# Graph network kernel on one core: the waits in front of the four row gathers of an edge chunk are exchanged

## The chip, the cores and the metric

The kernel runs on one core of one Trainium2 chip. The metric is the device time of one execution in microseconds (us). The kernel before takes 4315.86 us, the median of three runs (4311.51 to 4329.4).

## The reference

The model has four graph layers over 3125 nodes of 128 features and 50000 edges sorted by their end node. The change touches the first one, and of it the part that is computed for each edge. Cut to that part:

```python
x_src = node_features[src]
h = silu(edge_attr @ fc1 + b1);  h = silu(h @ fc2 + b2);  scale = h @ fc3 + b3
msg = silu(x_src @ W_node * scale + edge_sh @ W_sh)
alpha_in = concatenate([x_src[:, :64], node_features[dst, :64], edge_attr], -1)
a = silu(alpha_in @ aW1 + ab1);  a = silu(a @ aW2 + ab2);  a = a @ aW3 + ab3
```

The softmax over the edges, the sums over the edges of a node and the three later layers follow in later phases. They are not touched.

## The kernel before, in words

`edge_messages` is one phase of the kernel. It handles the edges in 100 chunks of 512 (`CE`), and four buffers (`U` = 4) hold the chunks in flight. An earlier phase has already computed, for every node, one row of 256 numbers in DRAM: `x @ W_node` and `x[:, :64] @ aW1[:64]`. For each chunk GpSimd copies the 512 edge ends from `idx` into `slot` (line 983, the operand named `em_idx`) and then issues four indirect DMAs (line 998), each of which gathers 128 rows of 1 KB into `gs[:, u, j]`, j = 0 to 3. They are called gather 0 to gather 3 here. Each raises `rows_in[u]`.

The other engines go through the chunks in turns. In turn c TensorE runs these steps in this order:

- `begin(c)`: the first edge layer FC1 (line 1021), the edge part of the score layer (1022), the product SH of the chunk before (1014), the part of the end nodes (1028) and the transposes of the gathered halves (1034), which complete the sum A1.
- `counts`: in one or two places of a turn six matmuls of line 1070, which count edges between node blocks for a later layer. Two turns in four have them twice, two once.
- `finish(c-1)`: SCALE (1043) and the score product A3 (1049).
- `middle(c)`: FC2 (1060) and A2 (1062). Then the scores of chunk c-1 are transposed (1055), then come the second `counts`.

ScalarE applies the four activations H1, A1, H2 and A2 (all at line 1106), the message MSG (1120) and the copies of the counts (1127). VectorE copies the scores out of PSUM (1189, `em_a`), and then adds b3 (TB, 1190), multiplies by the gathered rows (TG, 1193, the step after which `gs[:, u]` is free) and adds SH (TS, 1196). Beside that it builds one-hot matrices for the counts (1246, 1247). In the first 64 chunks it also splits 16 pieces of another edge input (1210, 1214).

Every step raises a semaphore. `early` is raised by TensorE after FC1, A1, FC2 and A2, `late` by TensorE after SH, SCALE and A3, `act_` by ScalarE after H1, A1, H2 and A2, `dve_` by VectorE after TB, TG, TS and the last score step, `scores_ok` by VectorE after line 1189. `X.of(c, "NAME")` is the value that the semaphore has once step NAME of chunk c is done. The next turn of TensorE begins when ScalarE has finished A2 of the chunk:

```python
def begin(c, u, i, fast, first=False):
    pe.wait_ge(feat_in[u // 2], (i + 1) * 48)
    pe.wait_ge(act_.sem, act_.of(c - 1, "A2"))
```

Each engine executes its instructions in order, so a wait on GpSimd holds up whatever gathers stand behind it. Nothing but the index copies and the gathers is on GpSimd in this phase. SyncE issues all the other DMAs of the phase from a queue of its own and waits for nothing that GpSimd does. `both` runs `body(True)` for inputs like these ("fast"); `body(False)` is a general path that is not executed here.

Of the kernel before, what the change touches and what calls it, by code (L numbers as in the profile page):

```python
# [782 lines left out]
def edge_messages(k, idx, a_all, first_, tops):  # L783
# [4 lines left out]
    U, NWI, NHI = NCU, NWU, NWU * NH  # L788
    EW_, SHW = 2 * EA, 2 * EA + SH
    pieces, step = PIECES, EW // GQ // PIECES  # L790
    with k.phase("em") as (sb, sem, block, hop):
# [20 lines left out]
        early = Steps(sem("early"), ["FC1", "A1", "FC2", "A2"], U)  # L812
        late = Steps(sem("late"), ["SH", "SCALE", "A3"], U)
        scores_turned = Steps(sem("scores_turned"), ["A3"], U)
        scores_ok = Steps(sem("scores_ok"), ["A3"], U)
        cleared, topped = sem("cleared"), sem("topped")
        act_ = Steps(sem("act"), ["H1", "A1", "H2", "A2"], U)
        act_msg = Steps(sem("act_msg"), ["MSG"], U)
# [4 lines left out]
        dve_ = Steps(sem("dve"), ["TB", "TG", "TS", "A3"], U)  # L823
        HB, AB, SCALE, SHB, A3, ADJ, HB2 = 0, 1, 2, 3, 4, 5, 7
# [19 lines left out]
        def both(eng, body):  # L844

            with eng.If(eng.value_load(k.fits[0:1, 0:1], min_val=0, max_val=1) == 1):
                body(True)
            with eng.If(eng.value_load(k.fits[0:1, 0:1], min_val=0, max_val=1) == 0):
                body(False)
# [125 lines left out]
        @block.gpsimd  # L975
        def _(pool):
            def body(fast):
                with pool.Fori(0, NC // U) as i:
                    for u in range(U):
                        c = U * i + u  # L980
                        pool.wait_ge(early.sem, early.of(c - U, "A1"))
                        pool.sem_inc(hop["pool"], 1)
                        nc.gpsimd.tensor_copy(slot[:, u, :].unsqueeze(1), idx[:, bass.ds(c, 1), :]).then_inc(indexed.sem, 1)
                        pool.wait_ge(dve_.sem, dve_.of(c - U, "TG"))
                        pool.sem_inc(hop["pool"], 1)
                        pool.wait_ge(indexed.sem, indexed.of(c, "IDX"))
                        pool.sem_inc(hop["pool"], 1)
                        for j in range(4):
                            if fast and j == 1:
                                pool.wait_ge(act_msg.sem, act_msg.of(c - U, "MSG"))  # L990
                                pool.sem_inc(hop["pool"], 1)
                            if fast and j == 2:
                                pool.wait_ge(act_.sem, act_.of(c - U + 2, "H1"))
                                pool.sem_inc(hop["pool"], 1)
                            if fast and j == 3:
                                pool.wait_ge(scores_ok.sem, scores_ok.of(c - U + 1, "A3"))
                                pool.sem_inc(hop["pool"], 1)
                            pool.indirect_dma_start(out=gs[:, u, j, :], out_offset=None, in_=d["rows0"],  # L998
                                                    in_offset=bass.IndirectOffsetOnAxis(ap=slot[:, u, 2 * j:2 * j + 1], axis=0)
                                                    ).then_inc(rows_in[u], 16)  # L1000
                            if not fast:
                                pool.indirect_dma_start(out=gd[:, u, j, :], out_offset=None, in_=d["rows0d"],
                                                        in_offset=bass.IndirectOffsetOnAxis(ap=slot[:, u, 2 * j + 1:2 * j + 2], axis=0)
                                                        ).then_inc(rows_in[u], 16)

            indexed.prime(pool)
            both(pool, body)

        @block.tensor
# [3202 lines left out]
```

## Time and profile before

| | |
|---|---|
| median of three runs | 4315.86 us |
| the profiled execution, its own time | 4329.4 us |
| its span, from the first to the last instruction | 4327.6 us |
| TensorE clock granted, mean of the span | 0.916 of full speed |
| the phase `edge_messages` | from 83 to 890 us of the span |

The profile is of one execution, the slowest of the three. Its own time is 1.8 us more than its span. Times in the rows below are microseconds from the start of the span. In a row of the timeline the bracket at the end gives how long the engine had been idle before the instruction, and what ended that idle time; "remote" and "issue" mean that the profile names no instruction. PE is TensorE, ACT is ScalarE, DVE is VectorE, POOL is GpSimd. The end of a PE row is modelled, and a row of several matmuls ("x8") gives the start of the first.

### The profile page before, as it was taken

The page shows a single profiled execution, that of the slowest core. Times are in us where ns is not written, and L with a number is a line of the kernel's source. Part 1 is how long each engine was busy: PE and PEld are TensorE (multiplying, and loading weights), DVE is VectorE, ACT ScalarE, POOL GpSimd, SP SyncE. Part 2 cuts the span into 40 slices and gives each one's busy share as a digit, 9 for nine tenths or more (in the row PEclk, how much of TensorE's full clock was granted, in tenths as well). Part 3 has the DMA queues.
Part 4 walks back from the last instruction along what each step waited for, and adds up shares of the span by engine and source line. Part 5 has one row for each costly group of instructions (what it writes and reads, how often), then busy time and mean ns, then how long its engine had stood idle before and what let it go on. Part 6 is the DMA issues. An engine that isn't in the chain of part 4 may idle for free. (4 is left out here: it accounts for less than half of the span.)

```text
span 4327.6 us, 82914 instructions
## 1 busy us (share of the span) xinstructions
PE 3495.6 (81%) x22381; PEld 2067.5 (48%) x22381; DVE 1823.4 (42%) x5369; ACT 1433.0 (33%) x3483; POOL 1862.8 (43%) x1907
## 2 busy tenths in 40 slices
PE   4999999947758888876777777667777769999998
PEld 2666666635534444443444444334443444555564
DVE  4666666647523333332333333323333323344222
ACT  3555555522623333332233323222222223122112
POOL 2555555500256665653566656456666630000000
PEclk8999999979879999998888998878898889999999
DMA  5677775656444554555666666556666645443223
GB/s 139 187 200 199 198 196 167 165 115 204 140 136 137 140 136 131 139 137 136 169 176 172 176 175 179 156 155 167 167 164 168 166 111 176 171 177 118 74 97 125
DMA packets 716528, 675.29 MB, mean 156 GB/s; under 512 B 382359, under 2 KB 542945, under 8 KB 716117
## 3 DMA queue, kind: packets, MB, share of 16 engines
q1 hardware_dynamic: 622598, 466.26, 37.1%
q0 software_dynamic: 77008, 200.24, 17.2%
q10 hardware_dynamic: 16768, 6.91, 0.6%
q8 instruction: 76, 1.25, 0.1%
q14 instruction: 78, 0.64, 0.0%
HBM read 530.84 MB, written 142.28 MB: 156 GB/s over the span
## 5 line engine op out<-in xcount | busy, mean ns | idle before, releaser
L2293 POOL DMA_INDIRECT l_y<-s_lrows,l_src x1344 | 1352.6, 1006 | 964.3 <-issue 352.4
L2373 PE MATMUL ps<-l_y,aw_pT 128*63 128x277 f32 x2700 | 436.8, 467 | 259.9 <-ACT aw_pT L2591 249.1
L3404 PE MATMUL ps<-nl_adj,nl_table 126*128 126x504 bf16 (+1 forms) x3150 | 631.4, 357 | 2.3 <-DVE nl_table L3639 2.3
L998 POOL DMA_INDIRECT em_gs<-s_rows,em_idx x400 | 432.3, 1081 | 325.8 <-DVE em_a L1189 147.9
L2357 PE MATMUL ps<-aw_yT,aw_qt 128*63 128x384 f32 x1800 | 377.2, 529 | 120.0 <-DMA aw_yT<-s_dxT 61.2
L3404 PEld LDWEIGHTS ps<-nl_adj,nl_table 126*128 126x128 bf16 x3150 | 301.8, 96 | 299.0 <-issue 5.3
L2750 DVE COPY aw_axd<-ps 128x252 f32<-128x252 f32 x225 | 94.7, 421 | 796.9 <-remote 409.9
L2330 PE MATMUL ps<-ident,l_y 128*128 128x128 f32 x1800 | 281.5, 292 | 150.9 <-issue 83.1
L2373 PEld LDWEIGHTS ps<-l_y,aw_pT 128*63 128x63 f32 x2700 | 195.7, 154 | 431.9 <-ACT aw_pT L2591 279.6
L2591 ACT ACTIVATE aw_pT<-ps 128x381 f32<-128x381 f32 x225 | 109.9, 488 | 736.8 <-remote 506.0
L2577 ACT ACTIVATE aw_yT<-ps 128x512 f32<-128x512 f32 (+1 forms) x525 | 261.4, 536 | 245.2 <-remote 114.7
L2330 PEld LDWEIGHTS ps<-ident,l_y 128*128 128x128 f32 x1800 | 220.5, 150 | 202.3 <-issue 124.5
L2730 DVE TENSOR_REDUCE aw_mx<-ps 127x1 f32<-127x384 f32 x225 | 124.5, 553 | 396.9 <-remote 333.0
L2599 ACT ACTIVATE aw_agr<-ps,aw_inv 127x277 f32<-127x277 f32 x225 | 111.0, 494 | 440.4 <-PE ps L2373 200.0
L2357 PEld LDWEIGHTS ps<-aw_yT,aw_qt 128*63 128x63 f32 x1800 | 108.8, 148 | 239.5 <-issue 92.0
L2715 DVE TENSOR_TENSOR l_y<-l_y 128x768 f32<-128x768 f32 x225 | 212.4, 944 | 24.1 <-issue 14.4
L1106 ACT ACTIVATE em_h<-ps,ei_bias 128x512 f32<-128x512 f32 x200 | 136.3, 682 | 147.3 <-PE ps L1060 79.0
L1247 DVE TENSOR_SCALAR em_oh_key<-ei_iota_key,em_key 128x546 bf16<-128x546 int16 x450 | 165.7, 368 | 0.0
L1106 ACT ACTIVATE em_a<-ps,ei_bias 128x512 f32<-128x512 f32 x200 | 137.2, 686 | 72.8 <-PE ps L1034 26.0
L2365 PEld LDWEIGHTS ps<-ident,aw_p 127*128 127x128 f32 x675 | 73.7, 147 | 145.1 <-issue 144.3
L2584 ACT ACTIVATE aw_p<-ps,aw_neg 127x384 f32<-127x384 f32 x225 | 132.4, 589 | 31.6 <-DVE aw_neg L2733 16.4
L1189 DVE COPY em_a<-ps 104x128 f32<-104x128 f32 x100 | 29.2, 292 | 251.0 <-remote 182.5
(381 smaller groups left out, 5866.1 us busy)
## 6 DMA issues: line engine op xcount, KB each, us to landing
nl_adj<-s_adj SPq DMA_DIRECT2D x20, 3100.8 KB
aw_yT<-s_dxT SPq DMA_DIRECT2D x150, 384.0 KB
aw_geoS<-s_geoS SPq DMA_DIRECT2D x450, 94.5 KB
nl_adj<-s_adj SPq DMA_DIRECT2D x15, 2325.6 KB
ws_msg<-s_msg SPq DMA_DIRECT2D x75, 384.0 KB, 3.8
s_dxT<-aw_yT SPq DMA_DIRECT2D x75, 384.0 KB
aw_qt<-s_qt SPq DMA_DIRECT2D x225, 126.0 KB
s_msg<-em_msg SPq DMA_DIRECT2D x100, 256.0 KB
```

Of the source, the lines that this page charges most:

```text
L998: pool.indirect_dma_start(out=gs[:, u, j, :], out_offset=None, in_=d["rows0"], in_offset=bass.IndirectOffsetOnAxis(ap=slot[:, u, 2 * j:2 * ...
L1106: nc.scalar.activation(to[:, u % 2, :], k.ps[:, bank, :], ACT.Silu, bias=bias[:, col:col + 1]).then_inc(act_.sem, 1)
L1247: nc.vector.tensor_scalar(oh_key[:, o, j, :], iota_key[:, :], key[:, v, q:q + 1], None, ALU.is_equal).then_inc(s, 1)
L2293: pool.indirect_dma_start(out=y[:, u, j, 0:W], out_offset=None, in_=table, in_offset=bass.IndirectOffsetOnAxis(ap=src[:, u, j:j + 1], axis ...
L2330: m = nc.tensor.transpose(k.ps[:, FEATURES[n], q * 128:(q + 1) * 128], y[:, u, j, what * D:(what + 1) * D], k.ident[:, :])
L2357: m = nc.tensor.matmul(rows_(v), qt[:, u, v, t, :], yT[:, SLOT[u], t, v * HS:(v + 1) * HS], start=False, stop=t == 1)
L2373: m = nc.tensor.matmul(k.ps[64 * v:64 * v + HW, SUM, 0:SW], pT[:, SLOT[u], j, 64 * v:64 * v + HW], y[:, u, v * TH + j, 0:SW], start=j == 0 ...
L2577: nc.scalar.activation(yT[:, SLOT[u], :, :].rearrange("p t s -> p (t s)")[:, n * 512:n * 512 + size], k.ps[:, FEATURES[n], 0:size], ACT.Co ...
L2584: nc.scalar.activation(p[:, SLOT[u], :], k.ps[0:M, SCORE[u], 0:HS], ACT.Exp, bias=neg[:, u:u + 1], scale=SCALE, accum_out=den[:, u:u + 1]) ...
L2715: nc.vector.tensor_tensor(y[:, u, :, D:2 * D], y[:, u, :, W - D:W], bc(y[:, u, :, G0:G0 + 1], [128, T, D]), ALU.mult).then_inc(ready.sem, 1)
L2730: nc.vector.tensor_reduce(mx[:, u:u + 1], k.ps[0:M, SCORE[u], 0:HS], AX.X, ALU.max).then_inc(s, 1)
L3404: m = nc.tensor.matmul(k.ps[:, bank(i, p), 0:cols * WN], source[:, p, q, b, :], adj[:, a % 2, 0:cols, b * WN:(b + 1) * WN], start=b == 0 a ...
```

## The change

The loop over the chunks on GpSimd keeps its index copy and its four gathers. What they wait for changes:

| in front of | before | after |
|---|---|---|
| the index copy of chunk c | A1 of c-4 (TensorE) | TG of c-4 (VectorE) |
| gather 0 | TG of c-4, own copy | own copy, H2 of c-3 (ScalarE) |
| gather 1 | MSG of c-4 (ScalarE) | nothing |
| gather 2 | H1 of c-2 (ScalarE) | FC1 of c-2 (TensorE) |
| gather 3 | the score copy of c-3 (VectorE, line 1189) | A1 of c-2 (TensorE) |

```diff
                         c = U * i + u
-                        pool.wait_ge(early.sem, early.of(c - U, "A1"))
+                        pool.wait_ge(dve_.sem, dve_.of(c - U, "TG"))
                         pool.sem_inc(hop["pool"], 1)
                         nc.gpsimd.tensor_copy(slot[:, u, :].unsqueeze(1), idx[:, bass.ds(c, 1), :]).then_inc(indexed.sem, 1)
-                        pool.wait_ge(dve_.sem, dve_.of(c - U, "TG"))
-                        pool.sem_inc(hop["pool"], 1)
                         pool.wait_ge(indexed.sem, indexed.of(c, "IDX"))
                         pool.sem_inc(hop["pool"], 1)
+                        if fast:
+                            pool.wait_ge(act_.sem, act_.of(c - U + 1, "H2"))
+                            pool.sem_inc(hop["pool"], 1)
                         for j in range(4):
-                            if fast and j == 1:
-                                pool.wait_ge(act_msg.sem, act_msg.of(c - U, "MSG"))
-                                pool.sem_inc(hop["pool"], 1)
                             if fast and j == 2:
-                                pool.wait_ge(act_.sem, act_.of(c - U + 2, "H1"))
+                                pool.wait_ge(early.sem, early.of(c - U + 2, "FC1"))
                                 pool.sem_inc(hop["pool"], 1)
                             if fast and j == 3:
-                                pool.wait_ge(scores_ok.sem, scores_ok.of(c - U + 1, "A3"))
+                                pool.wait_ge(early.sem, early.of(c - U + 2, "A1"))
                                 pool.sem_inc(hop["pool"], 1)
```

## Rows read from the trace of the kernel before

**Rows 1.** The page: the span, and TensorE's busy time, share and instructions.
```profile
span 4327.6 us, 82914 instructions
...
PE 3495.6 (81%) x22381; PEld 2067.5 (48%) x22381; DVE 1823.4 (42%) x5369; ACT 1433.0 (33%) x3483; POOL 1862.8 (43%) x1907
```

**Rows 2.** Busy time by stretch of 100 us: each engine, then clock, DMA share, GB/s.
```profile
750.00:850.00 100.00, 98.50 (x648) 63.59 (x647) 65.89 (x231) 52.19 (x84) 58.14 (x64) 1.00 0.58 168
```

**Rows 3.** The source line 1189: count, ns min/median/max, first and last start.
```profile
L1189 DVE COPY em_a<-ps x100: 291/292/293, 104.3 to 886.7; 104x128 f32<-104x128 f32 x100
```

**Rows 4.** Timeline of one turn amid the phase: start, us, engine, line [idle before].
```profile
813.46 0.29 DVE L1189 COPY em_a<-ps 104x128 f32<-104x128 f32 x1 [3.65 <-remote]
...
814.38 0.69 DVE L1193 TENSOR_TENSOR em_t<-em_t,em_gs 128x512 f32<-128x512 f32 x1
814.54 1.36 POOL L998 DMA_INDIRECT em_gs<-s_rows,em_idx  x1 [1.81 <-DVE em_a L1189]
...
814.82 0.69 PE L1021 MATMUL ps<-ei_feat,ei_fc 32*128 32x512 f32 x1
...
815.90 0.20 POOL L983 COPY em_idx<-idx_all 128x8 int32 x1
...
816.89 1.16 POOL L998 DMA_INDIRECT em_gs<-s_rows,em_idx  x1 [0.79 <-ACT em_msg L1120]
...
817.16 1.06 PE L1034 MATMUL ps<-ident,em_gs 128*128 128x128 f32 x8
...
818.25 0.69 ACT L1106 ACTIVATE em_a<-ps,ei_bias 128x512 f32<-128x512 f32 x1 [0.59 <-PE ps L1034]
...
818.35 1.09 POOL L998 DMA_INDIRECT em_gs<-s_rows,em_idx  x1 [0.30 <-issue]
...
819.74 0.95 POOL L998 DMA_INDIRECT em_gs<-s_rows,em_idx  x1 [0.30 <-issue]
...
819.75 0.41 PE L1049 MATMUL ps<-em_a,ei_aw 128*8 128x128 f32 x8
...
820.08 1.13 PE L1060 MATMUL ps<-em_h,ei_fc 128*128 128x512 f32 x2
...
821.37 0.29 DVE L1189 COPY em_a<-ps 104x128 f32<-104x128 f32 x1 [2.31 <-PE ps L1049]
...
821.41 0.69 ACT L1106 ACTIVATE em_h<-ps,ei_bias 128x512 f32<-128x512 f32 x1 [0.23 <-PE ps L1060]
...
822.85 0.69 PE L1021 MATMUL ps<-ei_feat,ei_fc 32*128 32x512 f32 x1
```

**Rows 5.** Timeline of a turn after the last gather of the phase (869.41).
```profile
869.99 0.66 PE L1021 MATMUL ps<-ei_feat,ei_fc 32*128 32x512 f32 x1
...
873.92 0.41 PE L1049 MATMUL ps<-em_a,ei_aw 128*8 128x128 f32 x8
...
874.25 1.12 PE L1060 MATMUL ps<-em_h,ei_fc 128*128 128x512 f32 x2
...
874.39 0.29 DVE L1189 COPY em_a<-ps 104x128 f32<-104x128 f32 x1 [2.05 <-PE ps L1049]
...
875.42 0.69 ACT L1106 ACTIVATE em_h<-ps,ei_bias 128x512 f32<-128x512 f32 x1 [1.59 <-PE ps L1060]
...
877.11 0.66 PE L1021 MATMUL ps<-ei_feat,ei_fc 32*128 32x512 f32 x1
```

**Rows 6.** Timeline of the second turn of the phase.
```profile
97.05 0.69 PE L1021 MATMUL ps<-ei_feat,ei_fc 32*128 32x512 f32 x1 [0.78 <-ACT em_a L1106]
...
101.06 0.41 PE L1049 MATMUL ps<-em_a,ei_aw 128*8 128x128 f32 x8
...
104.32 0.29 DVE L1189 COPY em_a<-ps 104x128 f32<-104x128 f32 x1 [9.48 <-remote]
```

**Rows 7.** Timeline of a turn in which VectorE also splits a piece.
```profile
404.53 0.71 DVE L1210 TENSOR_TENSOR em_edge_left<-ei_edge,em_edge_part 126x536 f32<-126x536 f32 x1
...
404.61 0.66 POOL L983 COPY em_idx<-idx_all 128x8 int32 x1
```

## The prediction

> **What bounds the kernel now.** The page comes first: TensorE is busy for 81% of the span [rows 1]. That is a mean over phases; the change lies in one phase, so the next view is the busy time by stretch. In the middle of the phase TensorE is busy for 98.5 of 100 us at a granted clock of 1.00, which is the 2.4 GHz level [rows 2]. By that row alone the phase is bound by TensorE, the gathers have no part in it, and the change could do nothing. But ends of PE rows are modelled, so I look at who receives TensorE's results. The score copy, line 1189, runs 100 times from 104.3 to 886.7 us [rows 3]: one turn in 782.4/99 = 7.90 us.
>
> The timeline of one turn shows what fills the 7.9 us [rows 4]. TensorE starts the score product, line 1049, at 819.75, and VectorE's copy of it starts at 821.37, 1.62 us later. TensorE starts FC2, line 1060, at 820.08, a third of a microsecond after, and ScalarE's H2 starts at 821.41, 1.33 us later. Two results that TensorE made one after the other arrive 0.04 us apart. In a turn without gathers the same two steps take 874.39-873.92 = 0.47 us and 875.42-874.25 = 1.17 us [rows 5]. So beside a row of gathers the completions of TensorE are seen late, the scores by 1.15 us, FC2 by 0.16 us in this turn. The turn itself is shorter without gathers: from line 1021 to line 1021 877.11-869.99 = 7.12 us [rows 5] against 822.85-814.82 = 8.03 us [rows 4]. The latter has one set of count matmuls more, some 0.7 us, so 0.2 us of it is the delay; in the turn ahead of it, without the additional set, far more is.
>
> The third thing to see is when they arrive: 821.37 is 0.68 us after the end of the last gather of a close row of three (818.35, 819.74 and the one at 816.89), 819.74+0.95 = 820.69 [rows 4]. And a row of gathers that is longer delays more: in the second turn of the phase, where all semaphores are still primed and GpSimd issues without pause, line 1049 starts at 101.06 and the copy at 104.32, 3.26 us later [rows 6]. A1, whose last transposes start at 817.16 before the second gather of the row, reaches ScalarE at 818.25, at once [rows 4]. My reading: a completion of TensorE that falls into the second or a later gather of a close row is held until some 0.7 us after the last one ends, or slips through between. Three turns is a small basis for the mechanism, but it closes a loop whose sum fits: copy start to gather 3 1.08 us (814.54-813.46), gather 1.36, index copy 0.20, hand-over 0.79, gathers 0 to 2 with their gaps 1.16+0.30+1.09+0.30+0.95 = 3.80, hold 0.68, together 7.91 us, and the next copy does start 7.91 us later (821.37-813.46) [rows 4]. GpSimd's own chain sets the turn, with 1.4 us of it in waits that it makes itself.
>
> At one point the Trainium skill speaks against this. Its page "SBUF — State Buffer", section "Who interferes with whom", says that only the port pair of VectorE and GpSimd causes contention and that TensorE and ScalarE wait for nobody. By that rule the gathers can't touch TensorE's turn and the sum of the change is nothing; by the rows it is what follows. The 1.15 us disagree with the rule for completions, if not for the matmuls themselves, and I follow the rows but leave the rule a chance.
>
> **The change, part by part.** Take the turn that starts at 814.82. TG, line 1193, ends at 814.38+0.69 = 815.07 [rows 4].
>
> 1. Gather 3 no longer waits for the score copy. Before it started 1.08 us after the copy and took 1.36 us beside line 1193 instead of the 0.95 us of another gather: 0.41 us of GpSimd's time comes back, and it is in the chain.
> 2. The index copy now waits for TG instead of A1 of four chunks ago. A1 was long done; TG ends 1.61 us after the score copy starts. So the chain has 1.61 us where it had 1.08, and the hand-over from TG to the index copy comes on top. No row shows this one. The bounds are 0 and the 0.79 us that a gather needs after what it waited for; the index copy is a short operation that follows without a DMA to prepare, so I take 0.3 us, nearer the lower.
> 3. The index copy was behind the gather and beside line 1210 in the 16 turns that split a piece: 0.66 us there instead of 0.20 [rows 7]. It now stands beside line 1196, which reads one of its inputs from PSUM. If it is undisturbed, 16 x 0.46 = 7 us are saved; if line 1196 holds it up as line 1210 did, all 96 turns cost 0.46 us more, 44 us. I take the saving.
> 4. H2 of c-3 in front of gather 0: it ends 0.69 us after its start and starts with the score copy [rows 4], before TG does. Nothing, plus at most 0.1 us for one more wait. The wait for MSG that goes was met already (gap 0.30 us before 818.35). FC1 for H1 at gather 2: both long done. Nothing either way, and their cover is the whole row of gathers.
> 5. Gather 3 waits for A1 of c-2, the transposes of line 1034 in the turn that is running. Now 0.30 us after gather 2 it would be ready if A1 has been seen. The four gathers then form one close row.
>
> The row would start at 815.07+0.3+0.20+0.79 = 816.36 and run 3.80 us to gather 2's end at 820.16, and with gather 3 (0.30+0.95) to 821.41. A3 of this turn (819.75 and 0.47) and FC2 fall inside, so both are held to 821.41+0.68 = 822.09. The new chain from score copy to score copy is 1.61+0.3+0.20+0.79+3.80+1.25+0.68 = 8.63 us against 7.91, +0.72 us a turn. With the bounds of step 2 it is 8.33 to 9.12. That is a **joined** turn.
>
> But A1 is a completion of TensorE too. Its transposes start at 817.16 and it is due at 818.25 [rows 4]. The second gather of the new row would start at 816.36+1.16+0.30 = 817.82, so A1 is due inside it and may be held. If it slips through by about 819.7, gather 3 joins. If not, it is freed at 820.16+0.68 = 820.84, and A3 with it, 0.53 us earlier than today; gather 3 starts another 0.79 us later, alone. FC2 is then not held at all. That is a **split** turn. Its lower bound is a turn without gathers: 7.12 us with one set of counts and about 7.8 with two, mean 7.48 against 7.90, -0.42. Since A1 itself comes late for ScalarE I take -0.3 us.
>
> Nothing else is behind the waits: GpSimd holds only the next gathers, and TensorE needs chunk c+3's rows some 11 us after they are issued, so late rows are no price. The number of turns is 96, from chunk 4 on; the first four are primed and nearly unchanged.
>
> **The forecast.** A joined turn releases scores and FC2 together, which puts the next TG late in its turn and A1 deep into the row: likely held. A split turn releases the scores early, TG comes early, A1 falls near the first gather and is seen at once: joined. So I expect both kinds in turn, somewhat more joined (11 in 20), since one that slips through is enough. 0.55 x 0.72 - 0.45 x 0.3 = +0.26 us a turn, x 96 = +25 us, less 7 us from step 3: +18 us. The profiled execution goes from 4329.4 to 4347 us. It lies 13.5 us above the median of the runs, so the median goes from 4315.9 to 4334 us.
>
> **The rivals.**
>
> - *Always joined.* A1 slips through each time, as completions in close rows sometimes must for the sum to close. 0.72 x 96 - 7 = +62 us: 4378 us. For it: the second turn of the phase, 3.26 us. Against: A1 is due half a microsecond into the second gather.
> - *Always split* (the other side). The place is gather 3 behind A1; it decides as soon as A1 is seen later than 0.79 us before gather 2's end plus the hold, about 820.1. -0.3 x 96 - 7 = -36 us: 4280 us, with the bound of -0.42 4268 us. For it: A3 in rows 4 was held for 1.15 us, and A1 held as long would be seen at 819.4, not far off. Against: a turn whose A1 is prompt ends it.
> - *No change.* TensorE's queue, 98.5% busy [rows 2], is the bound after all and late completions only show where it has slack. Then 4316 us, or 4309 with step 3. The page named above would give this case. Against: the 7.12 us turn.
> - *A blocked index copy.* With 44 us on top of the forecast 4385 us; unlikely, since it needs line 1196 to block.
>
> **How the numbers follow.** A measurement of this kernel tells about 0.5%, 21.6 us, from no change. Chances: mixed 0.30, always joined 0.24, always split 0.25, no change 0.17, blocked copy 0.04. The mixed case with shares from 0.4 to 0.7 joined runs from 4319 to 4348 us, so I split it into 0.03 faster, 0.15 within and 0.12 slower. Faster 0.28, within 0.32, slower 0.40. The likeliest case's own range is 4312 to 4355 us. The range for 8 in 10 reaches to both rivals: 4268 (split at its bound) to 4385 us.
>
> **What would show it.** The start of line 1189 against line 1049, per turn: over 2 us in joined turns, under 1.2 in split ones; below 0.5 everywhere would mean that the new places avoid the hold entirely. The mean turn, first to last start of line 1189 over 99: 8.1 to 8.2 for the forecast, 8.6 joined, 7.5 split, 7.9 no change. GpSimd: four gathers with gaps of 0.30 us, or a gap above 0.9 us before the fourth. Gather 3 at 0.95 us, not 1.36, shows step 1; an index copy of 0.20 us in all turns, step 3. A turn that is long although scores are prompt would show that my loop is the wrong one.

## The result and the profile after

The changed kernel takes 4390.31 us (median of 4 executions, 4382.59 to 4400.81) where the kernel before takes 4322.63 us (4 executions on the same chip). The ratio is 1.016, 95% interval 1.0124 to 1.0196: **slower by 1.6%**, outside the range of 4268 to 4385 us and on the side to which I had given 0.40. The profiled execution took 4409.3 us, with a span of 4407.5 us.

All line numbers of the phase behind 985 are two lower now: the gathers are 996, the score copy is 1187. Three views answer to [rows 1, 3]: the busy times of the page, two groups of the lines (busy us, mean ns, idle time before, and what ended it), and the score copy's line by itself (shortest, median and longest in ns, first and last start in us).

```profile
PE 3495.3 (79%) x22381; PEld 2087.8 (47%) x22381; DVE 1826.6 (41%) x5369; ACT 1429.6 (32%) x3483; POOL 1819.9 (41%) x1907
```

```profile
L996 POOL DMA_INDIRECT em_gs<-s_rows,em_idx x400 | 400.5, 1001 | 247.2 <-issue 86.0 <-PE ps L1058 59.9 <-ACT em_a L1104 46.5
L983 POOL COPY em_idx<-idx_all 128x8 int32 x100 | 19.1, 191 | 227.2 <-DVE em_t L1191 157.3 <-DVEq L69 55.8 <-issue 14.0
```

```profile
L1187 DVE COPY em_a<-ps x100: 291/292/293, 107.5 to 939.4; 104x128 f32<-104x128 f32 x100
```

TensorE is busy for the same 3495 us [rows 1]; nothing was added to its work. The score copy now runs from 107.5 to 939.4 us, one turn in 831.9/99 = 8.40 us instead of 7.90. That is 50 us of the loss, the whole of what the change can have done: in the attention phase, whose code is the same, the profiled execution of after took 29 us longer (2313.5 us against 2284.1 from the first to the last matmul of its line 2371, before 2373), but over the 14 profiled executions in this study with late reports that phase took 2284 to 2331 us, whatever the kernel. For the rest of the span, which I use below as a cleaner measure beside the ratio, before has 4327.6-2284.1 = 2043.5 us and after 2094.0 us.

A mean turn of 8.40 us hides two patterns. Cut at turn 67 (TensorE's FC1 to FC1, turn 0 is the first): in turns 2 to 66 the mean is 8.77 us where before has 7.98; in turns 68 to 97 it is 7.73, and before has 7.85. The windows show the granted clock of the two parts, from turn 3 to 66 and from 69 to 97 (window, length, busy us of PE, PEld, DVE, ACT and POOL, clock, DMA share, GB/s):

```profile
118.69:680.18 561.49, 511.46 (x3265) 336.80 (x3265) 348.23 (x1166) 274.95 (x447) 270.87 (x319) 0.94 0.64 180
698.81:923.36 224.55, 206.00 (x1484) 139.98 (x1483) 149.18 (x517) 116.35 (x190) 120.02 (x144) 0.98 0.61 169
```

This is the slow pattern, from the timeline of one joined turn. It began at 360.90 (line 1019) and the next at 369.78, so 8.88 us:

```profile
361.32 0.19 POOL L983 COPY em_idx<-idx_all 128x8 int32 x1 [2.96 <-DVE em_t L1191]
362.45 0.97 POOL L996 DMA_INDIRECT em_gs<-s_rows,em_idx  x1 [0.94 <-POOL em_idx L983]
363.16 1.06 PE L1032 MATMUL ps<-ident,em_gs 128*128 128x128 f32 x8
363.73 1.05 POOL L996 DMA_INDIRECT em_gs<-s_rows,em_idx  x1 [0.31 <-issue]
364.25 0.69 ACT L1104 ACTIVATE em_a<-ps,ei_bias 128x512 f32<-128x512 f32 x1 [0.60 <-issue]
365.08 0.95 POOL L996 DMA_INDIRECT em_gs<-s_rows,em_idx  x1 [0.30 <-issue]
365.74 0.41 PE L1047 MATMUL ps<-em_a,ei_aw 128*8 128x128 f32 x8
366.33 0.95 POOL L996 DMA_INDIRECT em_gs<-s_rows,em_idx  x1 [0.30 <-issue]
368.42 0.29 DVE L1187 COPY em_a<-ps 104x128 f32<-104x128 f32 x1 [2.57 <-remote]
...
370.28 0.19 POOL L983 COPY em_idx<-idx_all 128x8 int32 x1 [3.01 <-DVE em_t L1191]
```

A1 (line 1032, 363.16) reaches ScalarE 1.09 us later, at once; so gather 3 starts with the 0.30 us gap of an unhindered row, and the score product started at 365.74 is copied 2.68 us later. From one index copy to the next are 8.96 us: the next turn looks much the same (there A1 is seen after 2.25 us, still ahead of gather 2's end). All of this is from one profiled execution of each kernel. And this is the other pattern, a split turn of the last third, from 824.04 to 831.68 = 7.64 us:

```profile
824.58 0.99 POOL L996 DMA_INDIRECT em_gs<-s_rows,em_idx  x1 [0.94 <-ACT em_a L1104]
825.46 1.06 PE L1032 MATMUL ps<-ident,em_gs 128*128 128x128 f32 x8
825.88 1.07 POOL L996 DMA_INDIRECT em_gs<-s_rows,em_idx  x1 [0.30 <-issue]
827.25 1.10 POOL L996 DMA_INDIRECT em_gs<-s_rows,em_idx  x1 [0.30 <-issue]
828.05 0.40 PE L1047 MATMUL ps<-em_a,ei_aw 128*8 128x128 f32 x8
829.04 0.69 ACT L1104 ACTIVATE em_a<-ps,ei_bias 128x512 f32<-128x512 f32 x1 [3.15 <-remote]
829.30 0.29 DVE L1187 COPY em_a<-ps 104x128 f32<-104x128 f32 x1 [1.76 <-PE ps L1047]
829.79 0.95 POOL L996 DMA_INDIRECT em_gs<-s_rows,em_idx  x1 [1.44 <-PE ps L1058]
830.22 0.69 DVE L1191 TENSOR_TENSOR em_t<-em_t,em_gs 128x512 f32<-128x512 f32 x1
```

Here A1 is seen only 829.04-825.46 = 3.58 us later, 0.69 us behind the end of the third gather, and gather 3 comes apart. In turns 26, 52 and 78 GpSimd pauses for some 3 us ahead of gather 1, in every kernel here that has four gathers; these turns and the ones behind them (27, 53, 79) are left out of all counts of joined turns below. Of the other turns from 2 to 66, 47 have four gathers in a row (gather 3 less than 1.95 us behind gather 2), with a mean of 9.06 us; of those from 68 to 97 none has (78 and 79, at the pause, do).

With the turns at the pauses counted in, there are twelve stretches of joined turns. Eleven begin in a turn in which VectorE does the second subtraction of an edge piece, the twelfth at the pause in turn 78. One of the eleven:

```profile
415.68 0.69 PE L1019 MATMUL ps<-ei_feat,ei_fc 32*128 32x512 f32 x1
416.12 0.70 DVE L1212 TENSOR_TENSOR em_edge_part<-em_edge_left,em_edge_part 126x536 bf16<-126x536 f32 x1
416.21 1.45 POOL L996 DMA_INDIRECT em_gs<-s_rows,em_idx  x1 [0.94 <-ACT em_a L1104]
417.10 1.06 PE L1032 MATMUL ps<-ident,em_gs 128*128 128x128 f32 x8
417.97 1.13 POOL L996 DMA_INDIRECT em_gs<-s_rows,em_idx  x1 [0.30 <-issue]
418.19 0.69 ACT L1104 ACTIVATE em_a<-ps,ei_bias 128x512 f32<-128x512 f32 x1 [0.67 <-issue]
```

Gather 0 started 0.09 us behind the subtraction and took 1.45 us instead of 0.97 to 1.10. The second gather then starts late, A1 is seen at once, 0.22 us behind its start, and gather 3 joins. Of turns 3 to 97, 18 have a gap of over 1.6 us between the starts of gathers 0 and 1 (the three pauses among them), and in all 18 A1 is seen 1.09 us behind its transposes. The Trainium skill, page "SBUF — State Buffer", section "Who interferes with whom", says that a VectorE instruction with two inputs in SBUF contends with a GpSimd instruction that reads SBUF, and that the order of issue decides who is blocked. The trace agrees with the contention and with one side of the order: in [rows 4] a gather that started 0.16 us behind line 1193 took 1.36 us, and in the split turn above one that started 0.43 us ahead of the same operation took 0.95 us. The other side it doesn't show: VectorE's operation, which came second there (830.22), took the same 0.69 us as ever.

The last thing in the trace is the clock. Nine of turns 2 to 97 take over 10 us, eight of them up to turn 67; before has none. One is the turn from 396.93 to 408.18 (the windows of the turn before it, its own and the next):

```profile
387.95:396.93 8.98, 7.64 (x50) 4.66 (x49) 4.06 (x13) 4.21 (x7) 4.07 (x5) 1.00 0.48 143
396.93:408.18 11.25, 11.25 (x55) 7.95 (x54) 7.52 (x24) 4.48 (x8) 4.29 (x6) 0.70 0.55 152
408.18:415.68 7.50, 6.58 (x50) 4.38 (x49) 4.96 (x21) 4.14 (x8) 4.10 (x5) 1.00 0.60 175
```

After joined turns, in which TensorE is busy for only 7.64 of 8.98 us, the granted clock falls, for part of a turn, from the 2.4 to the 1.2 GHz level (0.70 is the mean of this one), and the turn takes 2.2 us more than a joined one does in the mean. Counted so, the nine turns are 20 us of the 50, an estimate. Such a turn mostly ends the pattern: here, as after most of them, the next is split. In turns 2 to 97 the clock stands at the 1.2 GHz level for 83 us of the changed kernel and for 9 us of before.

### The profile page after: what moved, and what is told of

The parts are those of the page before. It is cut to its first block and busy times, and to the rows that moved or that the text cites. A ratio compares the mean times of both kernels' runs of the same rounds, so it can differ in the third digit from the quotient of the medians.

```text
span 4407.5 us, 82939 instructions
## 1 busy us (share of the span) xinstructions
PE 3495.3 (79%) x22381; PEld 2087.8 (47%) x22381; DVE 1826.6 (41%) x5369; ACT 1429.6 (32%) x3483; POOL 1819.9 (41%) x1907
## 3 DMA queue, kind: packets, MB, share of 16 engines
q10 hardware_dynamic: 16768, 6.91, 0.6%
## 5 line engine op out<-in xcount | busy, mean ns | idle before, releaser
L2371 PE MATMUL ps<-l_y,aw_pT 128*63 128x277 f32 x2700 | 445.8, 475 | 287.7 <-ACT aw_pT L2589 283.9
L996 POOL DMA_INDIRECT em_gs<-s_rows,em_idx x400 | 400.5, 1001 | 247.2 <-issue 86.0
```

What stands on the lines that cost most here:

```text
L2371: m = nc.tensor.matmul(k.ps[64 * v:64 * v + HW, SUM, 0:SW], pT[:, SLOT[u], j, 64 * v:64 * v + HW], y[:, u, v * TH + j, 0:SW], start=j == 0 ...
```

## The experiments

The ratio is to the kernel before on the same chip, with its 95% interval. "Turn" is first to last score copy over 99. "Rest" is the profiled span without the attention phase. The first twelve ran where before takes 4328 to 4373 us; kernels 13 to 16 (13 was run three times) where it takes 3766 to 3768 us, more on that below. Turn and rest are of one profiled execution each. The times in my expectations for kernels 1 to 4 reckon with a before of 4323 us; where they ran it takes 4363 us.

| kernel | ratio | turn, us | rest, us |
|---|---|---|---|
| before | | 7.90 | 2043.5 |
| changed | 1.016 (1.0124-1.0196) | 8.40 | 2094.0 |
| 1 index copy behind TG alone | 1.000 (0.9985-1.0014) | 7.95 | 2048.5 |
| 2 gather 3 behind A1 alone | 0.9979 (0.9961-0.9996) | 7.79 | 2034.0 |
| 3 changed, short subtractions | 1.0027 (1.0008-1.0046) | 8.13 | 2062.5 |
| 4 changed, gather 3 behind FC2 | 0.9973 (0.9951-0.9994) | 7.85 | 2041.0 |
| 5 before, gather 3 behind FC2 | 0.9975 (0.996-0.9991) | 7.88 | 2043.6 |
| 6 parts 1 and 2 together | 0.9971 (0.9951-0.9992) | 7.80 | 2034.1 |
| 7 changed, no piece work | 1.0024 (1.0007-1.0041) | 8.04 | 2059.2 |
| 8 before, one gather a chunk | one execution, 4260.6 us | 6.77 | 1930.7 |
| 9 changed without the H2 wait | 0.9963 (0.9942-0.9985) | 7.70 | 2025.5 |
| 10 changed with H1 for FC1 | 1.0147 (1.0117-1.0177) | 8.48 | 2096.4 |
| 11 part 6 and a wait for MSG | 1.0326 (1.0287-1.0364) | 9.28 | 2176.3 |
| 12 part 2 without the MSG wait | 0.9988 (0.9957-1.0018) | 7.80 | 2035.4 |
| 13 as 9, one passed wait | 0.9996 (0.9973-1.0019) | 6.91 | 1925.5 |
| 14 as 9, three passed waits | 1.0014 (0.9993-1.0035) | 6.97 | 1930.8 |
| 15 as 9, gather 3 behind FC2 | 0.9985 (0.9968-1.0002) | 7.00 | 1932.7 |
| 16 as 9, rows of two | 0.9998 (0.9976-1.0019) | 6.99 | 1932.2 |

**The parts alone (1 and 2).** Kernel 1 is before with the two waits exchanged around the index copy:

```diff
-                        pool.wait_ge(early.sem, early.of(c - U, "A1"))
+                        pool.wait_ge(dve_.sem, dve_.of(c - U, "TG"))
...
-                        pool.wait_ge(dve_.sem, dve_.of(c - U, "TG"))
-                        pool.sem_inc(hop["pool"], 1)
```

> The kernel before with one part of the change alone: the index copy waits for the product TG and no longer for A1; the gathers keep their old waits. Theory H (TensorE's completion reports are held while gathers follow each other closely, and gather 3 in the same row as gathers 0 to 2 makes the row long): gather 3 still waits for the score copy and stands apart, so the phase keeps turns of 7.8 to 8.1 us and the time is 4310 to 4345 us. Rival C (the index copy and its hand-over, now in series behind TG, lengthen the chain by themselves): turns of about 8.4 us as in the changed kernel, 4365 to 4395 us.

Kernel 2 is before with

```diff
-                                pool.wait_ge(scores_ok.sem, scores_ok.of(c - U + 1, "A3"))
+                                pool.wait_ge(early.sem, early.of(c - U + 2, "A1"))
```

> The kernel before with another part alone: gather 3 waits for the matmul A1 of two chunks back in place of the score copy of three chunks back; index copy and gathers 0 to 2 as before. Theory H: gather 3 follows gather 2 by 1.3 us, rows of four, score copy 2.7 to 3.4 us behind its matmul, turns of 8.2 to 9.0 us, 4350 to 4430 us. Rival C (index copy): gather 3 merely comes earlier, no turn is longer than before, at or below 4323 us.

Kernel 1 made no difference, so the index copy in series is not by itself the loss (rival C falls). Kernel 2 was a miss for my theory as it then stood: rows of four do occur, in 36 of turns 2 to 66, with a mean of 8.30 us, but never in more than three turns on end, and in turns 68 to 97 the turn is 7.34 us. Gather 3 behind A1 is by itself a small gain.

**The edge pieces (3 and 7).** Kernel 3 is the changed kernel with the two subtractions on 8 of 536 columns; the others hold zeros:

```diff
-                nc.vector.tensor_tensor(edge_left[:, :], edge[:, :], edge_part[:, 0, :], ALU.subtract)
+                nc.vector.tensor_tensor(edge_left[:, 0:8], edge[:, 0:8], edge_part[:, 0, 0:8], ALU.subtract)
...
-                nc.vector.tensor_tensor(edge_part[:, 2, :], edge_left[:, :], edge_part[:, 1, :], ALU.subtract)
+                nc.vector.tensor_tensor(edge_part[:, 2, 0:8], edge_left[:, 0:8], edge_part[:, 1, 0:8], ALU.subtract)
```

> The changed kernel with VectorE's two subtractions of the edge pieces done on 8 of their 536 columns (work left out: two of the three parts of the edge features are zero elsewhere). Theory H with two patterns: in the changed kernel one of these subtractions delays gather 1 by 0.45 us, which lets A1's report through early, joins gather 3 to the row, and the pattern of four then keeps itself up. Without them the split pattern of the last 30 turns (7.64 us) holds in nearly all 98: 4280 to 4310 us. Rival C: nothing of the kind, the phase stays at 8.4 us a turn but for 16 times 0.7 us, 4370 to 4390 us. Rival D (TensorE's lower clock in these stretches is the cause, not the result): stretches at the lower clock stay, above 4350 us.

Kernel 7 is kernel 3 with ScalarE's two copies of a piece cut in the same way:

> The changed kernel with all four operations of the edge pieces, VectorE's two and ScalarE's two, on 8 of 536 columns (work left out: the split edge features are zero elsewhere). Theory H2: nothing but the missing gathers at turns 26 and 78 starts the pattern of four; it ends by itself; turns of 7.64 us in over 85 of 98, 4325 to 4350 us beside a before of about 4363. Rival (the pattern of four comes from something else that recurs, a store or a table load): about the 4376 us that VectorE's two alone gave.

With no change to a wait, the ratio fell from 1.016 to 1.003: joined turns went from 48 to 25 of 90, with all piece work short to 20. So the subtractions start most of the joined stretches of the changed kernel. But nothing of the kind is needed: both forecasts of a nearly clean phase were missed, and in kernel 7 stretches of joined turns also began in turns 13, 37, 66, 86 and others, where I found no operation that starts them. Eight of kernel 3's joined turns, and eight of kernel 7's, lie behind turn 67, where the changed kernel, with the same instructions there, has none; so that its last third was clean is in part luck.

**Gather 3 behind a later event (4 and 5).** The wait for A1 in the changed kernel (4), or for the score copy in before (5), becomes

```diff
+                                pool.wait_ge(early.sem, early.of(c - U + 2, "FC2"))
```

> The changed kernel with gather 3 behind the matmul FC2 of two chunks back in place of A1. Theory H: FC2's report always falls behind the row of three, so gather 3 never joins it, edge pieces or not; turns of 7.6 to 7.9 us, 4285 to 4325 us. Rival C: 4370 to 4395 us, as the index copy stands where it stood.

> The kernel before with gather 3 behind the matmul FC2 of two chunks back in place of the score copy; the index copy stays ahead of TG. Theory H2 (held reports; gather 0 directly behind TG with the copy already done, three gathers in a row, gather 3 apart in every turn because FC2's report always comes behind the row): turns near the 7.2 us that the same kernel with A1 in place of FC2 showed where it was not joined, in the edge-piece turns too: 4295 to 4330 us beside a before of about 4363 on this chip. Rival: FC2's report comes so late that gather 3 runs into the next gather 0; then 4 in a row again and 4355 to 4400 us.

Kernel 4 has no turn with gather 3 in the row of its own chunk and its ratio is 0.019 below the changed kernel's although index copy and H2 wait stand where they stood: with the row of four the loss is gone. A row of four is not a loss everywhere, though: kernels 2 and 12 have it in 36 and 45 of turns 2 to 66 and are no slower than before. Kernel 4 is about equal to before in its turns (7.85 us). Its gather 3, freed later, is followed within 2.3 us by gather 0 of the next chunk in 65 of 95 cases, with the index copy alone between them (the changed kernel: 2 of 95); that this takes the rest of the gain is argued, no run isolates it. In kernel 5 gather 3 does run into the next chunk's row: 28 of 96 turns have a close row of four, and the time lay above the range I gave.

**Which wait (6, 9, 10).** Kernel 6 puts parts 1 and 2 together. Kernels 9 and 10 are the changed kernel, without

```diff
-                        if fast:
-                            pool.wait_ge(act_.sem, act_.of(c - U + 1, "H2"))
-                            pool.sem_inc(hop["pool"], 1)
```

and with, at gather 2,

```diff
-                                pool.wait_ge(early.sem, early.of(c - U + 2, "FC1"))
+                                pool.wait_ge(act_.sem, act_.of(c - U + 2, "H1"))
```

> Index copy behind TG and gather 3 behind A1 of two chunks back together, with the kernel before's waits of gathers 1 and 2: the changed kernel without its H2 wait ahead of gather 0 and with H1 in place of FC1 ahead of gather 2. Theory H2 (the two harmless parts do their harm together: the copy in series puts gather 0 0.5 us later, so A1's report comes before the second gather and gather 3 joins the row): 4410 to 4440 us beside a before of about 4363, as the changed kernel's 1.016. Rival W (the new waits H2 and FC1 do it): 4350 to 4370 us.

> The changed kernel without its H2 wait ahead of gather 0, all else as changed (FC1 ahead of gather 2, A1 ahead of gather 3, copy behind TG). Theory T (a threshold in time: one more wait puts gather 0 0.15 us later, at +1.64 us of a joined turn in place of +1.49, which is enough for A1's report to come before the second gather, so that gather 3 joins the row again in the next turn): ratio to before 0.994 to 1.002. Rival F (FC1 in place of H1 ahead of gather 2 does it): ratio 1.010 to 1.018.

> The changed kernel with the old wait H1 ahead of gather 2 in place of FC1, the H2 wait kept. Theory T: ratio to before 1.008 to 1.018, as the changed kernel. Rival F: ratio 0.994 to 1.002.

Kernel 6 was a second miss: the two parts together are faster than before (0.9971). But it left only the new waits and the MSG wait that went, and two kernels that each differ from the changed one (1.016) in a single wait decide: **without the H2 wait the ratio is 0.9963, with it and H1 for FC1 it is 1.0147**. One wait on GpSimd (and the increment of `hop["pool"]` that stands behind it) is worth the whole loss and the small gain that the other parts would have brought. Kernel 9 beats both kernels; the ratios of kernels 2, 4, 5 and 6 lie within its interval.

What it does shows in the gap between the end of the index copy and gather 0: 0.78 to 0.85 us in the 100 turns of kernel 9, 0.93 to 1.02 us in those of the changed kernel, median 0.79 against 0.94. In 97 of its 100 turns the H2 that it waits for had ended before the index copy had. So it is hardly ever a late event; the wait costs 0.15 us in passing. What 0.15 us decide is seen in kernel 9's turn that began at 193.24:

```profile
193.73 0.19 POOL L983 COPY em_idx<-idx_all 128x8 int32 x1 [2.22 <-DVE em_t L1188]
194.71 0.97 POOL L993 DMA_INDIRECT em_gs<-s_rows,em_idx  x1 [0.79 <-POOL em_idx L983]
195.57 1.06 PE L1029 MATMUL ps<-ident,em_gs 128*128 128x128 f32 x8
195.98 0.95 POOL L993 DMA_INDIRECT em_gs<-s_rows,em_idx  x1 [0.30 <-issue]
197.24 1.05 POOL L993 DMA_INDIRECT em_gs<-s_rows,em_idx  x1 [0.30 <-issue]
198.28 0.69 ACT L1101 ACTIVATE em_a<-ps,ei_bias 128x512 f32<-128x512 f32 x1 [2.23 <-remote]
199.03 0.95 POOL L993 DMA_INDIRECT em_gs<-s_rows,em_idx  x1 [0.74 <-remote]
```

Both kernels start the transposes 1.84 us behind the start of the index copy in such a turn (195.57-193.73 and 363.16-361.32), since with a late TG the SH product ahead of them waits for VectorE too. But gather 0 starts 0.86 us ahead of the transposes here and 0.71 us in the changed kernel, and A1 is seen after 2.71 us in place of 1.09. Gather 3 still joins the row, 1.79 us behind gather 2, but the next turn is split.

This distance alone does not decide. A split turn of the last third in the changed kernel, the one that began at 816.38, has the same 0.71 us, and its A1 is held for 3.69 us:

```profile
817.00 0.98 POOL L996 DMA_INDIRECT em_gs<-s_rows,em_idx  x1 [0.94 <-ACT em_a L1104]
817.71 1.06 PE L1032 MATMUL ps<-ident,em_gs 128*128 128x128 f32 x8
821.40 0.69 ACT L1104 ACTIVATE em_a<-ps,ei_bias 128x512 f32<-128x512 f32 x1 [3.13 <-PE ps L1058]
```

Counted over all turns of the changed kernel whose gather 0 is not lengthened, gather 0 starts 0.65 to 0.85 us ahead of the transposes in 45 turns. Of these, 25 follow a turn with gather 3 in the row, and in 21 of the 25 A1 is seen within 2.3 us; 20 follow a split turn, and in none of the 20 is it. With 0.85 to 1.05 us it is 1 of 15, 6 of which follow a joined turn. So an early A1 took both here, a joined turn ahead and the short distance; what else the joined turn brings, beside the distance, these rows don't show. In kernel 9 the distance is 0.85 to 1.05 us in 77 turns, and none of them sees A1 so early. Its pattern of four therefore doesn't keep itself up: one joined turn (the one above) in 90, where the changed kernel has 48. That also means that only a few of its turns follow a joined one, so the test of the distance in kernel 9 is thin.

The wait costs in split turns too: in turns 68 to 97, where neither kernel has a joined turn away from the pause, kernel 9 takes 7.40 us a turn and the changed one 7.73. That is 10 us of the 68.5 us between their rests; the other turns, 7.90 against 8.77 us in turns 2 to 66, are 57.

**A wait that is really late (11), and one wait less (12).** Kernel 11 is kernel 6 with a wait for the message of four chunks back ahead of gather 0. Kernel 12 is kernel 2 without the wait for that message ahead of gather 1.

> The kernel with the copy behind TG and gather 3 behind A1 (ratio 0.997) with one more wait ahead of gather 0, on the message of four chunks back, an event long past, so that the wait costs only its own passage. Theory T (the later start alone, not what is waited for): ratio to before 1.008 to 1.018. Rival (the event H2 is what matters, since it holds gather 0 back behind ScalarE's queue in some turns): ratio 0.995 to 1.000.

> The kernel before with gather 3 behind A1 of two chunks back and without the wait for the message ahead of gather 1 (an event long past). Theory T: gather 1 starts 0.1 to 0.15 us sooner, the row ends sooner, no joined turns are added; ratio to before 0.992 to 0.998, a version that beats both. Rival: the sooner row makes A1's report fall where it lets gather 3 join, ratio 1.000 to 1.010.

I had the event of kernel 11 wrong. The message of c-4 is made from the very TG that the index copy waited for; it is about 1 us late, not long past. Gather 0 starts 1.88 us behind the index copy, 89 of 90 turns are joined, and the mean of turns 2 to 97 is 9.38 us. As a test of the passage it is void; as a larger dose it fits: +0.15 us of gather 0 cost 2.0% (changed against 9), +1.1 us 3.6% (11 against 6). Kernel 12 brought nothing that can be told from kernel 2 (one of its ten executions took 10786 us, which I can't explain), so neither the forecast of kernel 12 nor its rival is borne out.

**Is it the gathers at all (8)?** Before, with gather 0 alone:

```diff
-                        for j in range(4):
+                        for j in range(1 if fast else 4):
```

TensorE's wait for the rows is cut to one gather to match, and zeros stand in place of the rows of the other three.

> The kernel before with gather 0 alone of each chunk's four (work left out: three quarters of the gathered rows are zero). Theory H: a gather that stands alone holds no report, so the score copy comes 0.47 us behind its matmul's start and A1's activation about 1.1 us behind in every turn, and a turn is 7.0 to 7.2 us, about the 7.12 of the turn with no gather. Rival (reports are late for another reason, such as DMA traffic or ScalarE's order): turns of 7.6 us or more, score copy over 1 us behind.

A1 is seen within 1.15 us in all of turns 2 to 97, and the score copy is 0.47 us behind its product in 84 of the 96; in the others VectorE was busy. The turn is 6.77 us, shorter than the 7.0 to 7.2 I expected. Here turns take 6.30 us with one set of counts and 7.01 to 7.11 with two where VectorE is in time. The turn without gathers of [rows 5], 7.12 us, has one set, so as a floor it was 0.82 us too long: it came behind a turn with gathers, whose late scores still held up the SH product and with it the transposes, 872.04-869.99 = 2.05 us behind its start. In a turn of kernel 8 with one set they stand at 677.28-675.96 = 1.32 us. The line of before:

```profile
872.04 1.06 PE L1034 MATMUL ps<-ident,em_gs 128*128 128x128 f32 x8
```

The two of kernel 8:

```profile
675.96 0.69 PE L1021 MATMUL ps<-ei_feat,ei_fc 32*128 32x512 f32 x1
677.28 1.06 PE L1034 MATMUL ps<-ident,em_gs 128*128 128x128 f32 x8
```

The late reports of the rows cost the kernel before 7.90-6.77 = 1.13 us a turn. Kernel 8 alone can't tell the gathers on GpSimd from the transfers that they make, since it leaves out both; kernel 13 below has all of both and no late report, and its turns have the same 6.30 and 7.01 to 7.11 us.

**Passed waits and rows of two (13 to 16).** All are kernel 9 with: one more wait for TG of four chunks back, which has certainly passed (13, run three times: 0.9996, 0.9998 and 0.9994); three of them (14); gather 3 behind FC2 (15); gather 2 behind A1 and gather 3 directly after it (16).

> The changed kernel without its H2 wait (ratio 0.9963), with one more wait ahead of gather 0 on TG of four chunks back, which the index copy already waited for, so it has passed for certain and costs only its own passage. Theory T (threshold in time): gather 0 starts 0.1 to 0.2 us later, joined turns keep themselves up in the first two thirds, ratio to before 1.008 to 1.018. Rival E (the event H2 matters, a passed wait costs nothing that counts): ratio 0.994 to 1.000.

> As the run with one passed wait, with three of them. Theory T: gather 0 another 0.2 to 0.3 us later than with one, joined turns everywhere, the last third too; ratio 1.015 to 1.035. Rival E: 0.994 to 1.002.

> The changed kernel without its H2 wait and with gather 3 behind FC2 in place of A1: four gathers in a row are forbidden. Theory T: no turn of 9 us but at the two pauses of GpSimd; ratio 0.990 to 0.997. Rival: FC2's report comes so late that gather 3 runs into the next chunk's gather 0, ratio 0.997 to 1.005.

> The changed kernel without its H2 wait, gather 2 behind A1 of two chunks back and gather 3 directly after it: two rows of two in place of three and one. Theory H (reports that fall in the second or a later gather of a row are held to its end): A1's activation comes about 1 us sooner than behind a row of three, but the second row holds FC2's or A2's report to about +6.9 us of the turn; turns 7.2 to 7.9 us, ratio 0.985 to 1.005. Rival (no holding by rows; only how late the last gather is counts): the last gather ends no later than it did, so the ratio stays within 0.994 to 0.999 and the latencies as they were.

> The same kernel as the one with one passed wait ahead of gather 0, run again. Where the kernel before takes about 4320 to 4375 us (reports held beside gathers), theory T: gather 0 0.1 to 0.2 us later than without it, joined turns in the first two thirds, ratio to before 1.008 to 1.018. Rival E (a passed wait costs nothing that counts, the event H2 matters): 0.994 to 1.000. Where the kernel before takes about 3766 us: no held reports, ratio 0.997 to 1.002 and nothing told apart.

> The same kernel with one passed wait ahead of gather 0, a third time. Where the kernel before takes 4320 to 4375 us, theory T: ratio to before 1.008 to 1.018, joined turns in the first two thirds. Rival E: 0.994 to 1.000. Where it takes about 3766 us: 0.997 to 1.002, nothing told apart.

None of the six runs tells the theories apart, for a reason that I had not foreseen when I wrote the first four: they ran where **no report is late** (A1 within 1.15 us in 95 of turns 2 to 97 of kernel 13), and where the kernel before takes 3766 us, 13% less. This turn of kernel 13 has four gathers in a row:

```profile
669.57 0.69 PE L1019 MATMUL ps<-ei_feat,ei_fc 32*128 32x512 f32 x1
669.88 0.97 POOL L996 DMA_INDIRECT em_gs<-s_rows,em_idx  x1 [0.88 <-DVE a_all L1197]
670.89 1.06 PE L1032 MATMUL ps<-ident,em_gs 128*128 128x128 f32 x8
671.16 0.94 POOL L996 DMA_INDIRECT em_gs<-s_rows,em_idx  x1 [0.31 <-issue]
671.98 0.69 ACT L1104 ACTIVATE em_a<-ps,ei_bias 128x512 f32<-128x512 f32 x1 [0.57 <-PE ps L1032]
672.41 1.07 POOL L996 DMA_INDIRECT em_gs<-s_rows,em_idx  x1 [0.30 <-issue]
673.48 0.41 PE L1047 MATMUL ps<-em_a,ei_aw 128*8 128x128 f32 x8
673.78 0.94 POOL L996 DMA_INDIRECT em_gs<-s_rows,em_idx  x1 [0.30 <-issue]
673.95 0.29 DVE L1187 COPY em_a<-ps 104x128 f32<-104x128 f32 x1 [1.29 <-PE ps L1047]
...
676.58 0.69 PE L1019 MATMUL ps<-ei_feat,ei_fc 32*128 32x512 f32 x1
```

A1 is seen after 1.09 us and the scores after 0.47, in a turn of 7.01 us, and the gathers take what they took. A close row of four is thus not enough to make a report late. The rest of the span, 1922 to 1933 us, is that of kernel 8 where reports are held (1930.7). The order of the waits is then worth nothing: all ratios hold 1.000 in their interval. The runs gave one number more: gather 0 starts 0.79 us behind the index copy with no passed wait (16), 0.88 with one, 1.08 with three, so a passed wait (with its increment of `hop["pool"]`) costs about 0.1 us there.

## Why the prediction was wrong, step by step

- **What bounds the kernel.** Right in kind. Late reports beside rows of gathers set the turn, not TensorE's 98% of busy time: kernel 8 has the same TensorE work in 6.77 us. The page of the Trainium skill named in the prediction would have had no change at all; where reports are late, the measured turns with and without rows disagree with it for the reports, and where none is (kernels 13 to 16) they agree with it.
- **Step 1**, gather 3: right. The mean gather went from 1081 to 1001 ns.
- **Step 2**, TG and hand-over to the index copy: 0.25 us measured (median of 100 turns), 0.3 taken. In kernel 1 this part costs nothing that can be measured.
- **Step 3**, index copy: right. Its mean went from 292 to 191 ns. The adverse bound of 44 us did not come.
- **Step 4** is the term that was mis-sized: "nothing, plus at most 0.1 us for one more wait" for H2. It took 0.15 us, which is close, but I added it to a sum, where it was worth next to nothing, and did not ask where the 0.15 us puts gather 0. The changed kernel against kernel 9, with kernel 10 as a check, shows that the whole of the loss hangs on that wait. That it is its passage and not the event rests on the gaps in the trace; the runs that were to show it fell where no report is held, so this stays argued, and no run isolates the 0.15 us from anything else that the wait may do.
- **Step 5**, the two kinds of turn: the split turn was forecast at 7.6 us and took 7.6 to 7.7 in most of the last third. The bound under it, 7.12 us with one set of counts, was no floor: kernel 8 has 6.30. The joined turn was forecast at 8.63 and took 9.06 in the mean. The term that was too small is the hold, 0.68 us from the end of the row to the score copy, which I had read off one turn: in before's 90 turns it is 0.84 us in the median, in the 48 joined turns 1.10.
- **The forecast** is the step that failed: a joined turn "puts the next TG late in its turn and A1 deep into the row: likely held", so the kinds should alternate. The rows show the opposite: in the changed kernel 21 of 25 turns behind a joined one saw A1 early again, and none of 20 behind a split one did, at the same distance of gather 0 to the transposes. I moved the gathers with TG and left A1 where it was; but behind a late TG the SH product and with it the transposes move as well, so A1 keeps its distance to gather 0, 0.71 us, and it can be seen before the row is through: a joined turn mostly makes the next one joined. With the 0.86 to 0.94 us of kernel 9 it did not, in the few turns there that can tell. After a split turn TG is early, gather 0 starts at +0.54 to +0.64 us of TensorE's turn and 0.71 to 0.88 us ahead of the transposes, A1 is held, and the next turn is split. Why it is held there at 0.71 us too stays open. Each pattern keeps itself up, and a disturbance picks one. In the first two thirds the edge pieces disturb, and 47 of 61 turns are joined; behind them all but those at the pause are split, and there the change does save 0.12 us a turn.
- **The size.** (8.77-7.98) x 65 = +51 us in turns 2 to 66 and (7.73-7.85) x 30 = -4 us behind them. The rival *always joined* comes near with +62 us, but by accident: its turns are too short, half as many occur, and the turns of over 10 us at TensorE's lower clock are not in it. The medians differ by 68 us, 17 more than the phase; over the attention phase's own spread of 47 us I can't assign them.

## What to carry to other kernels

A sum of durations gives the length of a loop only if its events keep their places. Where a wait may or may not be met in time, work out for each outcome where it puts the same event in the *next* turn: if it moves it further to its own side, there can be two patterns that keep themselves up, and a tenth or two of a microsecond or one neighbour's operation picks between them. So a wait that has nearly always passed is worth taking out when it stands ahead of such a point, and the mean turn should be read by stretches before it is explained.

## What was not expected of the hardware

- Completions of TensorE beside close rows of gathers were late in before, the changed kernel and kernels 1 to 7 and 9 to 12 (the scores in mean 1.5 to 2.6 us behind their product in turns 2 to 97, in place of 0.47), and not late in the six runs of kernels 13 to 16, beside the same gathers at the same spacing. The kernel before takes 4316 to 4373 us in the one case and 3766 in the other; the attention phase, about 2300 and 1830 us, accounts for most of it. What differs between the two is not known from these runs; the chip's number in the record is no help, since it is 12 for kernels 9 to 12 and for kernels 13 to 16.
- The pattern of late turns takes TensorE to its 1.2 GHz level in places, though its work is the same: for 83 us of turns 2 to 97 in the changed kernel and 170 us in kernel 11, where 89 of 90 turns are joined and reports late, against 9 us in before. Single turns of this kind, 3 to 17 us at that level in all, occur in kernels 13 to 16 as well.
- A wait that has passed, with the increment behind it, took 0.15 us on GpSimd in the changed kernel and about 0.1 us in kernels 13 and 14. In kernel 4, with the same H2 wait as the changed kernel, gather 0 starts 0.88 us behind the index copy in the median, not 0.94; why is not known.
